# A graph network in three passes over the edges: first and second pass both with 15 sorted blocks and 44 gathered groups instead of 14 and 48

## The chip, the cores and the metric

The kernel runs on one core of a Trainium2 chip. Its five engines work side by side and wait for each other only through semaphores: TensorE (PE, matrix products into PSUM), VectorE (DVE), ScalarE (ACT), GpSimd (POOL, which here issues the gathers), and SyncE (SP, which issues all other transfers). The metric is the device time of one execution in microseconds; the kernel before has a median of 1861.92 us over three runs (1856.38 to 1866.67).

## The reference

There are 6250 nodes with 128 features and 106,250 directed edges, sorted by destination; each edge has one of 16 types. Cut to what matters:

```python
h = relu(layernorm(x))
for W, b in ((W1, b1), (W2, b2)):            # first and second pass over the edges
    s = segment_sum(h[src] @ W.T + b, dst);  h = s / max(count(dst), 1)
    h = relu(h) if W is W1 else h
x = x + h
h = relu(layernorm(x))
m = relu(concat(h[src], emb[type]) @ msg_W.T + msg_b)      # third pass
a = segment_sum(m, dst) / max(count(dst), 1)
x = x + layernorm(h + a @ upd_W.T + upd_b) * ln_g + ln_b
```

## The kernel before

**Edges, groups and blocks.** The sorted edges are padded to 104 groups of 1024. Each of the three passes has to fetch, for every edge, the row of its source node, and to sum these rows by destination. It does so in two ways at once. The first `NB[layer]` blocks of four groups (4096 edges) are sorted by the 128-node tile of their source, so that PE can pick the rows out of the node table in SBUF (`htab`) with a one-hot matrix. The remaining `NG[layer]` groups are gathered from a table in HBM by POOL. `NB = (14, 14, 13)` and so `NG = (48, 48, 52)`; `FIRST`, `OFF`, `GOFF` follow from them.

**A block.** It has `BUCKETS` = 52 buckets, one for each of 49 source tiles and 3 for what spills over, dealt out to `U` = 8 units of 7 or 6 buckets. For each bucket PE multiplies a one-hot of 128 sources (`src_hot`) with a tile of `htab` (`pick`: 384 columns, since a row is kept as three bf16 parts that add up to its fp32 value), ACT copies the result out of PSUM (L1135, tile `picked` in `region_a`), and PE sums it by destination with three products of 256 columns (`slot_sum`). DVE makes the one-hots of sources (L2038) and destinations (L1590 in the first pass, L2051 after), and at the end of a block adds its window of 256 destinations to `agg` (`last_adds`, `window_add`, L1989). There are four PSUM slots for picks.

**Sorting.** It is done once, in the first pass: while block b is summed, the tables of block b+1 and b+2 are made (`sort_*`, `digits_of`) by DVE, with small products on PE (`sort_before`, `sort_table`, `sort_turn`, `block_digits`, `block_count`) and one large copy on ACT (`tile_rows`, L1108, before the evacuations of unit 3). SP stores a block's codes (`store_codes`) to `src_tab` and `type_tab`, from which every pass loads them (L670). Edges that do not fit a block's window or buckets, or a group's window, are marked in `far` by a chain of DVE instructions after the last block of the first pass (L2138 to L2194). If any is marked, a fallback over all groups runs (the `If` branches); on these inputs none is.

**A gathered group.** POOL issues 8 indirect DMAs of 128 rows (`gather`, L829) into one of two buffers. It may start group k when the sum of group k-2 is done (`summed`). PE multiplies the rows with a one-hot of the destinations (8 x 3 products, in the first pass 8 more for the counts), DVE adds the window of 128. Group k has its place at the end of unit `place(layer, k) = (k+1) * NB * U // NG - 1` of the pass, so groups are spread evenly over the blocks. All engines' programs are written out in this order and follow it strictly.

**Early units.** The nodes are divided into 14 units of 4 or 3 tiles for the work after a pass. `early_units` lets a unit start during the second and third pass as soon as the blocks or groups that can reach it are behind: 10 of 14 in the second pass, each with products, transposes and products on PE spread over 8 units of the schedule (`early_products`), and copies on ACT (`early_sources`) and DVE (`early_rows`). The four others come after the pass. The third pass starts when the tables made there are complete: POOL needs the table in HBM, PE needs `htab`, which SP loads in part from `parts_tab` (L740).

Of the kernel before, what the change touches and what calls it, by code (L numbers as in the profile page):

```python
# [25 lines left out]
P = 128  # L26
C = 8
# [8 lines left out]
def gnn_program(nc, N, x, src, dst, first_dst, etype_cols, etype, W1T, b1, W2T, b2, embT, msgWT, msg_b,  # L36
# [16 lines left out]
    NB = (B + 1, B + 1, B)  # L53
    OFF = (0, B + 1, 2 * (B + 1))
# [4 lines left out]
    BLOCK_COLS = (B + 1) * BLOCK_C  # L59
# [17 lines left out]
    K3 = 3  # L77

    ctx = ExitStack()
    with ctx:  # L80
# [6 lines left out]
        def sems(name, n):  # L87
# [9 lines left out]
        src_tab = nc.dram_tensor("src_tab", (B + 1, BUCKETS, P), bf16, kind="Internal").ap()  # L97
        type_tab = nc.dram_tensor("type_tab", (B + 1, BUCKETS, P), bf16, kind="Internal").ap()
# [52 lines left out]
        type_f = sb("type_f", [P, 3, F])  # L151
        type_p = sb("type_p", [P, K3, F], bf16)
# [6 lines left out]
                 for h in hot]  # L159
        src_in = [sb(f"src_in{s}", [P, J * P], bf16) for s in range(2)]  # L160
# [418 lines left out]
        def _(sp):  # L579
# [96 lines left out]
            for layer in range(LAYERS):  # L676
                def step(b, first):
                    c = Count(sp, layer, b, first)
                    for u in range(U):
# [19 lines left out]
                        if layer == 0 and u == U - 1 and b < B:  # L699
                            store_codes(b + 1, b + 2)  # L700
# [76 lines left out]
            sp.wait_ge(code_T_stored, 32 * (B + 1))  # L777
# [126 lines left out]
        def _(act):  # L904
# [216 lines left out]
            for layer in range(LAYERS):  # L1121
                def step(b, first):
                    c = Count(act, layer, b, first)
                    for u in range(U):
                        if layer == 0 and u == 3 and b + 2 <= B:
# [44 lines left out]
        def _(pe):  # L1170
# [126 lines left out]
            for layer in range(LAYERS):  # L1297
# [37 lines left out]
                def step(b, first):  # L1335
# [3 lines left out]
                    for u in range(U):  # L1339
# [18 lines left out]
                        if layer == 0 and u == 5 and b < B:  # L1358
# [109 lines left out]
        def _(dve):  # L1468
# [66 lines left out]
            def split_over_partitions(value, p0, p1, p2, f0, f1, mask, to):  # L1535
# [17 lines left out]
            types_i = far[:, 0:BLOCK_COLS].bitcast(i32)  # L1553
            block_src, block_rel = src_all[:, 0:BLOCK_COLS], rel[:, 0:BLOCK_COLS]
# [14 lines left out]
                    lambda: V.tensor_tensor(float_c[:, 0:BC], dst_all[:, B * BC:(B + 1) * BC],  # L1569
                                            base_all[:, FIRST_GROUP:FIRST_GROUP + 1].broadcast_to([P, BC]), ALU.subtract),  # L1570
                    lambda: V.tensor_copy(rel_last[:, :], float_c[:, 0:BC]),
                    lambda: V.tensor_single_scalar(float_c[:, 0:BC], rel_last[:, :], 0.0, op=ALU.is_ge),
                    lambda: V.scalar_tensor_tensor(out=float_c[:, 0:BC], in0=rel_last[:, :], scalar=float(WIN_B - 1),
                                                   in1=float_c[:, 0:BC], op0=ALU.is_le, op1=ALU.mult),
                    lambda: V.scalar_tensor_tensor(out=codes[:, 1, B * BC:], in0=rel_last[:, :], scalar=1.0,
                                                   in1=float_c[:, 0:BC], op0=ALU.add, op1=ALU.mult),
# [402 lines left out]
            for layer in range(LAYERS):  # L1979
# [43 lines left out]
                def main(b, first):  # L2023
# [56 lines left out]
                    for u in range(U):  # L2080
# [10 lines left out]
                        if layer == 0:  # L2091
                            if u == 0:
                                if b < B:
                                    own = sort_codes(b + 1, 0)
                                make_digit_hot(b)
                            elif u == 1 and b < B:
                                sort_codes(b + 1, 1, own)
                                if b + 2 <= B:
                                    sort_tiles(b + 2)
                            elif u == 2 and b < B:  # L2100
# [253 lines left out]
```

## Time and profile before

| | |
|---|---|
| median of three runs | 1861.92 us |
| profiled execution | 1866.55 us |
| its span, first to last instruction | 1864.8 us |
| mean granted clock of TensorE, share of full | 0.969 |
| busy: PE | 1618.7 us (87%) |
| busy: DVE | 1365.2 us (73%) |
| busy: POOL | 1292.3 us (69%) |
| busy: ACT | 982.2 us (53%) |
| first pass, first to last matmul of a block | 93.1 to 652.6 us |
| second pass | 696.0 to 1206.4 us |
| third pass, from its first matmul | 1243.6 us on |

Matmuls are pipelined, so a busy PE need not be at its peak. Waits are named by what ended them. "issue" before a gather is the time between two instructions of POOL in which the profile shows no wait.

### The profile page before, as it was taken

What the parts mean: (1) busy time and instruction counts of PE and PEld (TensorE: products, weight loads), DVE (VectorE), ACT (ScalarE), POOL (GpSimd) and SP (SyncE); (2) the same over time, 40 slices, a digit from 0 to 9 for tenths busy, and PEclk for the clock granted to TensorE, in tenths of its full rate; (3) what the DMA queues carried; (4) which work ended last, traced back from release to release, by engine and by line L of the source; (5) the groups of instructions that cost most, each with busy time, mean ns of one, the idle gap of its engine ahead of it and who ended that gap; (6) DMA issues with size and microseconds to landing.
All of it is one profiled execution on the core that took longest, in us unless ns stands there. A gap on an engine that the chain in (4) does not pass through costs nothing.

```text
span 1864.8 us, 42446 instructions
## 1 busy us (share of the span) xinstructions
PE 1618.7 (87%) x15761; PEld 1377.4 (74%) x15761; DVE 1365.2 (73%) x3742; ACT 982.2 (53%) x1951; POOL 1292.3 (69%) x1318
## 2 busy tenths in 40 slices
PE   0189989989999967999999899849999999999996
PEld 0067777877777755777777777648998988899895
DVE  6767878878887463566666666467788888898886
ACT  3656666757766545777777777532222222222322
POOL 2087777777777617777777777657777776677772
PEclk9999999999999978999999999959999999999998
DMA  3334434344444336445555555636566666666662
GB/s 107 121 97 115 119 107 112 107 116 123 119 114 111 104 115 182 129 130 142 161 142 144 150 136 150 168 118 171 172 198 174 171 189 170 174 175 182 176 171 76
DMA packets 160332, 262.92 MB, mean 141 GB/s; under 512 B 30949, under 2 KB 126775, under 8 KB 160119
## 3 DMA queue, kind: packets, MB, share of 16 engines
q1 hardware_dynamic: 109944, 157.28, 28.6%
q0 software_dynamic: 50176, 102.84, 21.8%
q8 instruction: 130, 2.13, 0.5%
q14 instruction: 82, 0.67, 0.1%
HBM read 236.89 MB, written 23.11 MB: 139 GB/s over the span
## 4 chain that ended last, share of the span: by engine, by line
POOL 28%; PE 16%; issue 12%; DVE 4%; DMA 3%; ACT 1%; DVEq 0%; POOLq 0%
POOL rows L829 28%; PE banks L1172 16%; DMA rows<-table,src_all 3%; DVE region_a L2051 1%; DVE region_a L2257 0%; DVE htab L2262 0%; DVE agg L1989 0%; POOL region_b L842 0%; DVE rows L2077 0%; DVE x_or_cnt L1775 0%; DVE src_hot L2038 0%; DVE region_b L1976 0%; DVE stats L1800 0%; DVEq L1983 0%; DVE region_b L2036 0%
## 5 line engine op out<-in xcount | busy, mean ns | idle before, releaser
L829 POOL DMA_INDIRECT rows<-table,src_all x1184 | 1236.5, 1044 | 479.1 <-issue 440.1
L1172 PE MATMUL banks<-region_a 128*128 128x256 bf16 (+2 forms) x6168 | 1018.6, 291 | 2.3 <-DVE region_a L1590 2.3
L1135 ACT ACTIVATE region_a<-banks 128x384 bf16<-128x384 f32 x1456 | 671.7, 500 | 326.8 <-PE banks L1172 326.5
L1172 PEld LDWEIGHTS banks<-region_a 128*128 128x128 bf16 (+2 forms) x6168 | 691.8, 118 | 154.7 <-issue 4.7
L1172 PE MATMUL banks<-htab,src_hot 128*128 128x128 bf16 (+2 forms) x3484 | 631.6, 267 | 65.5 <-DVE src_hot L2038 32.9
L1172 PEld LDWEIGHTS banks<-htab,src_hot 128*128 128x128 bf16 x3484 | 288.7, 99 | 123.3 <-ACT region_a L1135 45.5
L1172 PE MATMUL banks<-hot,rows 128*128 128x128 bf16 (+1 forms) x3136 | 254.9, 239 | 63.1 <-DMA rows<-table,src_all 56.7
L1172 PEld LDWEIGHTS banks<-hot,rows 128*128 128x128 bf16 (+1 forms) x3136 | 240.8, 125 | 76.5 <-issue 54.3
L2038 DVE TENSOR_SCALAR src_hot<-src_in,part_no 128x768 bf16<-128x768 bf16 (+1 forms) x328 | 147.8, 452 | 130.6 <-PE banks L1172 115.4
L2051 DVE TENSOR_SCALAR region_a<-columns,slot_dst 128x256 f32<-128x256 f32 x676 | 210.6, 378 | 0.0
L1142 ACT ACTIVATE region_a<-banks 128x896 f32<-128x896 f32 (+1 forms) x104 | 88.9, 855 | 192.2 <-PE banks L1172 186.6
L1172 PE MATMUL banks<-type_rows,region_b 128*128 128x128 bf16 x1092 | 179.5, 221 | 0.8 <-DVE region_b L1976 0.7
L1989 DVE TENSOR_TENSOR agg<-agg,banks 128x128 f32 (+1 forms) x189 | 58.9, 312 | 159.3 <-PE banks L1172 115.9
L2051 DVE TENSOR_SCALAR region_a<-columns_b,slot_dst 128x256 bf16<-128x256 bf16 x728 | 155.4, 298 | 18.3 <-PE banks L1172 18.0
L1147 ACT ACTIVATE rows<-rows 128x1024 f32<-128x1024 f32 x52 | 55.0, 1057 | 200.8 <-DVE rows L2077 200.8
L2077 DVE TENSOR_TENSOR rows<-banks,rows 128x1024 f32<-128x1024 f32 x52 | 63.6, 1224 | 95.4 <-PE banks L1172 50.4
L1590 DVE TENSOR_TENSOR region_a<-columns_b,slot_dst 128x1792 bf16<-128x1792 bf16 (+1 forms) x112 | 113.8, 1016 | 10.5 <-PE banks L1172 10.5
L1172 PEld LDWEIGHTS banks<-type_rows,region_b 128*128 128x128 bf16 x1092 | 93.5, 99 | 7.0 <-DVE region_b L1976 1.5
L1590 DVE TENSOR_TENSOR hot<-columns_b,rel_pairs 128x1024 bf16<-128x1024 bf16 x96 | 65.5, 682 | 0.0
L1768 DVE TENSOR_TENSOR hot<-columns,rel 128x1024 f32<-128x1024 f32 x52 | 64.8, 1246 | 0.0
L1612 DVE TENSOR_TENSOR_SCAN region_b<-region_b 128x442 f16<-128x442 f16 (+1 forms) x56 | 54.0, 1007 | 2.3 <-ACT region_b L1108 2.2
L2036 DVE TENSOR_SCALAR region_b<-region_b,type_no 128x896 bf16<-128x896 bf16 (+1 forms) x104 | 53.6, 515 | 1.6 <-DMA region_b<-type_tab 1.6
(214 smaller groups left out, 1080.0 us busy)
## 6 DMA issues: line engine op xcount, KB each, us to landing
src_in<-src_tab SPq DMA_DIRECT2D x164, 224.0 KB, 3.4
src_in<-src_tab SPq DMA_DIRECT2D x164, 192.0 KB
region_b<-in_etype SPq DMA_DIRECT2D x52, 512.0 KB, 6.0
rows<-table,src_all POOLq DMA_INDIRECT x1184
region_b<-type_tab SPq DMA_DIRECT2D x52, 224.0 KB, 5.3
region_b<-type_tab SPq DMA_DIRECT2D x52, 192.0 KB
table<-htab SPq DMA_DIRECT2D x14, 384.0 KB, 3.4
table<-htab SPq DMA_DIRECT2D x14, 288.0 KB, 3.6
```

The source lines that it names most:

```text
L829: nc.gpsimd.indirect_dma_start(out=to[:, c, :], out_offset=None, in_=tab[layer], in_offset=bass.IndirectOffsetOnAxis(ap=cols[:, c:c + 1], ...
L1135: nc.scalar.activation(picked[u % 2][:, j, :], pick_ps[t % 4], ACT.Copy)\
L1142: nc.scalar.activation(messages[u % 2][:, 0:m, :], message_ps[u % 2][:, 0:m, :], ACT.Relu)\
L1147: nc.scalar.activation(rows_f[gi % 2], rows_f[gi % 2], ACT.Relu).then_inc(msgs_ready[gi], 1)
L1172: return nc.tensor.matmul(to, left, right, start=start, stop=stop)
L1590: return V.tensor_tensor(twos(to), twos(numbers), pairs.unsqueeze(2).broadcast_to([P, n, size // 2, 2]), op)
L1612: steps.done(V.tensor_tensor_scan(flat(ranks_ext[:, own, :]), flat(scan_mask[:, 0:own.stop - own.start, :]), flat(tile_ext[:, own, :]), 0. ...
L1768: return V.tensor_tensor(to, (columns if layer == 2 else columns_b)[:, :].unsqueeze(1).broadcast_to([P, C, P]), cols.unsqueeze(2).broadcas ...
L1989: V.tensor_tensor(agg[:, window], agg[:, window], ps, ALU.add).then_inc(added, 1)
L2038: V.tensor_scalar(src_hot[s][:, 0:m * P], src_in[s][:, 0:m * P], part_no[:, 0:1], None, ALU.is_equal)\
L2051: last = V.tensor_scalar(to[u % 2][:, j, :], numbers[:, :], slot_dst[:, b * BUCKETS + t:b * BUCKETS + t + 1], None, ALU.is_equal)
L2077: V.tensor_tensor(rows_f[gi % 2], type_ps, rows_f[gi % 2], ALU.add).then_inc(pre_ready[gi], 1)
```

## The change

The number of sorted blocks is 15 in the first and in the second pass (`NB = (B + 2, B + 2, B)`), so 44 groups are gathered in each, and the places of the groups follow. What was written for one block beyond the 13 common ones (`B + 1`) is written for `EXTRA` = 2 of them: the tables, the destinations relative to a block's first node (`rel_last`), and the marks of far edges. Two scratch tiles of the setup (`type_f`, `type_p`) move into halves of `hot` that the first two passes do not use, which makes room. ACT waits once, before the second table is made, for the last stored codes.

```diff
-    NB = (B + 1, B + 1, B)
-    OFF = (0, B + 1, 2 * (B + 1))
+    NB = (B + 2, B + 2, B)
+    OFF = (0, NB[0], NB[0] + NB[1])
+    SORTED = max(NB)
+    EXTRA = SORTED - B
...
-    BLOCK_COLS = (B + 1) * BLOCK_C
+    BLOCK_COLS = SORTED * BLOCK_C
...
-        slot_dst = sb("slot_dst", [P, (B + 1) * BUCKETS])
+        slot_dst = sb("slot_dst", [P, SORTED * BUCKETS])
...
-        rel_last = sb("rel_last", [P, BLOCK_C])
-        far_block = sb("far_block", [P, BLOCK_C])
-        far_group = sb("far_group", [P, BLOCK_C])
+        rel_last = sb("rel_last", [P, EXTRA * BLOCK_C])
+        far_block = sb("far_block", [P, EXTRA * BLOCK_C])
+        far_group = sb("far_group", [P, EXTRA * BLOCK_C])
...
-        type_f = sb("type_f", [P, 3, F])
-        type_p = sb("type_p", [P, K3, F], bf16)
...
+        type_f = hot[0][:, C // 2:C // 2 + 3, :]
+        type_p = hot[1][:, C // 2:C, :].rearrange("p c f -> p (c f)").bitcast(bf16)[:, 0:K3 * F].rearrange("p (k f) -> p k f", f=F)
...
+                        elif layer == 1 and b >= NB[0] and u == 0:
+                            sp.wait_ge(code_T_stored, 32 * (b + 1))
...
             def make_rows():
 
                 act.wait_ge(rinv_ready, 1)
+                act.wait_ge(code_T_stored, 32 * SORTED)
...
-                        if layer == 0 and u == 2 and b + 2 <= B:
+                        if layer == 0 and u == 2 and b + 2 < SORTED:
                             sort_before(b + 3)
-                        if layer == 0 and u == 3 and b < B:
+                        if layer == 0 and u == 3 and b + 1 < SORTED:
                             sort_table(b + 2)
...
-                here = rel_last[:, :] if b == B else rel[:, b * BC:(b + 1) * BC]
+                here = rel_last[:, (b - B) * BC:(b - B + 1) * BC] if b >= B else rel[:, b * BC:(b + 1) * BC]
...
-                    own, beyond = mask[:, 0:BC], spare[:, 0:BC]
-                    chained(lambda: V.tensor_copy(far_group[:, :], far[:, last]),
+                    own, beyond = mask[:, 0:EXTRA * BC], spare[:, 0:EXTRA * BC]
+                    now = (NB[0] - B) * BC
+                    chained(lambda: V.tensor_copy(far_group[:, :], far[:, extra]),
...
-                            lambda: V.tensor_copy(far[:, last], far_block[:, :]),
+                            lambda: V.tensor_copy(far[:, B * BC:B * BC + now], far_block[:, 0:now]),
```

The queue of POOL from the start of its first gathers to the end of the first pass; a gather is an indirect DMA of 128 rows, `x_or_cnt` holds the counts. Before, and then with the change:

```order
L829 DMA rows<-table,src_all 128x384 x16
L870 MEMSET x_or_cnt 128x6528
L829 DMA rows<-table,src_all 128x384 x368
L874 TENSOR_LOAD flag
L874 ISA x2
```

```order
L833 DMA rows<-table,src_all 128x384 x16
L874 MEMSET x_or_cnt 128x6528
L833 DMA rows<-table,src_all 128x384 x336
L878 TENSOR_LOAD flag
L878 ISA x2
```

32 gathers, four groups, are gone; the clearing of the counts still stands behind the second group.

PE in the first block of the first pass, from the sorting product of unit 3 (128x104) on. `hot,ones_b` is a group's count and `hot,rows` its sum; `htab,src_hot` is a pick and `region_a 128x256` the slot sums of a bucket; `region_a,ones` is the block's count at unit 4. Before:

```order
L1172 MATMUL banks<-region_b 128x104 x32
L1172 MATMUL banks<-hot,ones_b 128x128 x8
L1172 MATMUL banks<-hot,rows 128x128 x24
L1172 MATMUL banks<-htab,src_hot 128x384
L1172 MATMUL banks<-region_a 128x256 x3
```

With the change, the same product, and then the end of unit 4:

```order
L1177 MATMUL banks<-region_b 128x104 x32
L1177 MATMUL banks<-htab,src_hot 128x384
L1177 MATMUL banks<-region_a 128x256 x3
...
L1177 MATMUL banks<-region_a 128x256 x6
L1177 MATMUL banks<-region_a,ones 128x256
L1177 MATMUL banks<-hot,ones_b 128x128 x8
L1177 MATMUL banks<-hot,rows 128x128 x24
```

The second group has moved from the end of unit 3 to the end of unit 4; the groups of the first two blocks stood at units 1, 3, 6, 8, 10, 13, 15 and stand at 1, 4, 7, 9, 12, 15.

PE in the second pass, at the end of its fourth block. `w,agg` are the products that open an early unit; `TENSOR_LOAD first_tile` begins the next block. Before:

```order
L1172 MATMUL banks<-w,agg 128x128 x4
L1172 MATMUL banks<-hot,rows 128x128 x24
L1172 MATMUL banks<-region_a 128x256 x18
L1337 TENSOR_LOAD first_tile
L1337 ISA x2
L1172 MATMUL banks<-htab,src_hot 128x384 x7
L1172 MATMUL banks<-wm,region_b 128x128 x4
```

With the change:

```order
L1177 MATMUL banks<-hot,rows 128x128 x24
L1177 MATMUL banks<-region_a 128x256 x18
L1342 TENSOR_LOAD first_tile
L1342 ISA x2
L1177 MATMUL banks<-htab,src_hot 128x384 x7
L1177 MATMUL banks<-wm,region_b 128x128 x4
```

The early unit that opened here (number 8, four tiles) is no longer early and is done after the pass; unit 12, also of four tiles, is early instead and opens at unit 107 of 120. The numbers of early units, 10 in the second pass and 11 in the third, stay.

## Rows read from the trace of the kernel before

**Rows 1.** Windows of the two passes: stretch, length, busy us per engine, PEclk, DMA share, GB/s.

```profile
93.10:652.60 559.50, 523.53 (x5750) 422.94 (x5748) 436.92 (x939) 372.94 (x740) 433.93 (x381) 0.98 0.41 112
...
696.00:1206.40 510.40, 462.41 (x4239) 371.86 (x4239) 302.65 (x1173) 368.20 (x813) 382.35 (x384) 0.98 0.54 146
```

**Rows 2.** Waits in the first pass: who waited for what, us in total, times, longest.

```profile
POOL rows L829 <- issue: 115.7, 380, 0.3
PE banks L1172 <- DMA rows<-table,src_all: 17.4, 11, 3.2
```

**Rows 3.** Waits in the second pass.

```profile
POOL rows L829 <- issue: 125.0, 384, 8.2
PE banks L1172 <- DMA rows<-table,src_all: 39.3, 22, 7.5
```

**Rows 4.** Windows of instructions on the gathered rows, from the third group on, and second pass.

```profile
116.90:644.00 527.10, 73.43 (x1104) 66.90 (x1104) 0.00 (x0) 0.00 (x0) 413.87 (x368) 0.98 0.42 114
697.90:1197.10 499.20, 75.02 (x1128) 69.37 (x1128) 0.00 (x0) 0.00 (x0) 382.35 (x384) 0.98 0.54 146
```

**Rows 5.** Timeline of PE, first pass: start, us, engine, line, operation.

```profile
308.88 0.62 PE L1172 MATMUL banks<-hot,ones_b 128*128 128x128 bf16 x8
...
310.68 0.33 PE L1172 MATMUL banks<-htab,src_hot 128*128 128x384 bf16 x1
...
311.17 0.33 PE L1172 MATMUL banks<-htab,src_hot 128*128 128x384 bf16 x1
```

**Rows 6.** Timeline of DVE: adds of finished blocks in the first pass.

```profile
183.50 0.42 DVE L1989 TENSOR_TENSOR agg<-agg,banks 128x256 f32 x1 [1.48 <-PE banks L1172]
...
221.42 0.42 DVE L1989 TENSOR_TENSOR agg<-agg,banks 128x256 f32 x1 [1.45 <-PE banks L1172]
...
265.62 0.42 DVE L1989 TENSOR_TENSOR agg<-agg,banks 128x256 f32 x1 [1.51 <-PE banks L1172]
...
302.82 0.42 DVE L1989 TENSOR_TENSOR agg<-agg,banks 128x256 f32 x1 [1.42 <-PE banks L1172]
...
574.80 0.42 DVE L1989 TENSOR_TENSOR agg<-agg,banks 128x256 f32 x1 [0.56 <-issue]
...
611.38 0.42 DVE L1989 TENSOR_TENSOR agg<-agg,banks 128x256 f32 x1 [1.47 <-PE banks L1172]
```

**Rows 7.** Windows at low clock, end of first and start of second pass (PEclk 0.50).

```profile
634.80:641.60 6.80, 5.95 (x39) 4.66 (x40) 0.49 (x2) 1.47 (x3) 5.08 (x6) 0.50 0.30 80
...
733.80:740.50 6.70, 5.34 (x36) 4.31 (x37) 0.29 (x1) 1.32 (x3) 4.87 (x7) 0.50 0.95 289
```

**Rows 8.** Timeline of DVE: adds of finished blocks in the second pass.

```profile
745.02 0.42 DVE L1989 TENSOR_TENSOR agg<-agg,banks 128x256 f32 x1 [1.10 <-PE banks L1172]
...
776.91 0.42 DVE L1989 TENSOR_TENSOR agg<-agg,banks 128x256 f32 x1 [2.04 <-issue]
...
847.64 0.42 DVE L1989 TENSOR_TENSOR agg<-agg,banks 128x256 f32 x1 [1.69 <-PE banks L1172]
...
883.31 0.42 DVE L1989 TENSOR_TENSOR agg<-agg,banks 128x256 f32 x1 [1.21 <-PE banks L1172]
...
917.16 0.42 DVE L1989 TENSOR_TENSOR agg<-agg,banks 128x256 f32 x1 [1.87 <-PE banks L1172]
```

**Rows 9.** Groups by line and shape, PE, second pass.

```profile
L1172 PE MATMUL banks<-wm,region_b 128*128 128x128 f32 x70 | 9.4, 275 | 0.0
```

**Rows 10.** Timeline of DVE after the last block of the first pass.

```profile
654.84 0.18 DVE L2165 COPY far_group<-far 128x32 f32<-128x32 f32 x1
...
658.16 0.27 DVE L2188 TENSOR_TENSOR region_b<-region_b,limits 128x104 f32<-128x104 f32 x1
```

**Rows 11.** Timeline of SP and PE, end of second pass and start of third.

```profile
1203.56 4.86 SPq L740 DMA_DIRECT2D htab<-parts_tab  x10
...
1243.63 0.50 PE L1172 MATMUL banks<-htab,src_hot 128*128 128x128 bf16 x3 [3.73 <-DVE src_hot L2038]
```

**Rows 12.** The page, costliest groups: evacuations on ACT.

```profile
L1135 ACT ACTIVATE region_a<-banks 128x384 bf16<-128x384 f32 x1456 | 671.7, 500 | 326.8 <-PE banks L1172 326.5
```

More of the change, by code:

```diff
@@ L698, in step @@
                             sp.dma_start(xres, x_v).then_inc(x_in, 16)
-                        if layer == 0 and u == U - 1 and b < B:
+                        if layer == 0 and u == U - 1 and b + 1 < SORTED:
                             store_codes(b + 1, b + 2)
@@ L776, in _ @@
                 sp.wait_ge(out_stored[k], 16 * len(range(k, NV, 3)))
[L777 removed]
+            sp.wait_ge(code_T_stored, 32 * SORTED)
         @block.gpsimd
@@ L1124, in step @@
                     for u in range(U):
-                        if layer == 0 and u == 3 and b + 2 <= B:
+                        if layer == 0 and u == 3 and b + 2 < SORTED:
                             tile_rows(b + 3)
@@ L1357, in step @@
                             block_count(b)
-                        if layer == 0 and u == 5 and b < B:
+                        if layer == 0 and u == 5 and b + 1 < SORTED:
                             sort_turn(b + 2)
@@ L1568, in _ @@
                                                    op0=ALU.add, op1=ALU.mult),
[L1569 to L1576, printed above, removed]
+                    lambda: V.tensor_tensor(by_block(float_c[:, 0:EXTRA * BC]), by_block(dst_all[:, extra]),
+                                            first_of_block(base_all), ALU.subtract),
+                    lambda: V.tensor_copy(rel_last[:, :], float_c[:, 0:EXTRA * BC]),
+                    lambda: V.tensor_single_scalar(float_c[:, 0:EXTRA * BC], rel_last[:, :], 0.0, op=ALU.is_ge),
+                    lambda: V.scalar_tensor_tensor(out=float_c[:, 0:EXTRA * BC], in0=rel_last[:, :], scalar=float(WIN_B - 1),
+                                                   in1=float_c[:, 0:EXTRA * BC], op0=ALU.is_le, op1=ALU.mult),
+                    lambda: V.scalar_tensor_tensor(out=codes[:, 1, extra], in0=rel_last[:, :], scalar=1.0,
+                                                   in1=float_c[:, 0:EXTRA * BC], op0=ALU.add, op1=ALU.mult),
                     lambda: V.memset(scan_mask, 1.0),
@@ L2168, in _ @@
                                                            op0=ALU.is_gt, op1=ALU.max),
-                            lambda: V.scalar_tensor_tensor(out=far_block[:, :], in0=rank1[:, last], scalar=float(2 * P),
+                            lambda: V.scalar_tensor_tensor(out=far_block[:, :], in0=rank1[:, extra], scalar=float(2 * P),
                                                            in1=far_block[:, :], op0=ALU.is_gt, op1=ALU.max),
-                            lambda: V.tensor_tensor(own, tile_no[:, last, 0], first_tile[:, FIRST_GROUP:FIRST_GROUP + 1]
-                                                    .broadcast_to([P, BC]), ALU.subtract),
+                            lambda: V.tensor_tensor(by_block(own), by_block(tile_no[:, extra, 0]), first_of_block(first_tile), ALU.subtract),
                             lambda: V.tensor_single_scalar(beyond, own, 0.0, op=ALU.is_lt),
@@ L2175, in _ @@
                                                            op0=ALU.is_gt, op1=ALU.max),
-                            lambda: V.scalar_tensor_tensor(out=beyond, in0=rank1[:, last], scalar=float(P), in1=beyond,
+                            lambda: V.scalar_tensor_tensor(out=beyond, in0=rank1[:, extra], scalar=float(P), in1=beyond,
                                                            op0=ALU.is_gt, op1=ALU.mult),
                             lambda: V.tensor_tensor(far_block[:, :], far_block[:, :], beyond, ALU.max),
-                            lambda: V.scalar_tensor_tensor(out=own, in0=dst_all[:, last], scalar=1.0, in1=far_block[:, :],
+                            lambda: V.scalar_tensor_tensor(out=own, in0=dst_all[:, extra], scalar=1.0, in1=far_block[:, :],
                                                            op0=ALU.add, op1=ALU.mult),
                             lambda: V.tensor_single_scalar(far_block[:, :], own, -1.0, op=ALU.add),
-                            lambda: V.tensor_copy(far[:, last], far_block[:, :]),
+                            lambda: V.tensor_copy(far[:, B * BC:B * BC + now], far_block[:, 0:now]),
                             lambda: V.reduce_max(far_max[:, 1:2], far_block[:, :], axis=AX.X),
@@ L2206, in _ @@
                     if layer == 2:
-                        V.tensor_copy(far[:, B * BC:(B + 1) * BC], far_group[:, :]).then_inc(far_swapped, 1)
+                        V.tensor_copy(far[:, extra], far_group[:, :]).then_inc(far_swapped, 1)
                         dve.wait_ge(far_swapped, 1)
```

33 lines of the change are left out of this document (18 added, 15 removed).

## The prediction

> **What bounds the kernel now.** I read the busy times of the two stretches that the change touches, then who waits for whom in each, and last the timelines of TensorE (PE) and of VectorE (DVE). The matmuls of the first pass fill 559.5 us of the profile and those of the second 510.4 us, with PE, the busiest engine, at work for 94% and 91% of it [rows 1]. The reader is to see a second engine without slack beside PE: in both passes GpSimd (POOL) waits for nothing between its gathers but 0.3 us of its own issue, 380 and 384 times (the one of 8.2 us stands before the first gather of the second pass) [rows 2, 3]. A group of 8 gathers takes 527.1/46 = 11.5 us in the first pass and 499.2/48 = 10.4 us in the second [rows 4]. So POOL sets the pace of the passes as a whole: the 48 groups need 48 times that, and PE, which is nearly as slow, catches up with them and waits, 17.4 us in the first pass [rows 2] and 39.3 us in the second [rows 3]. Some of these waits cost twice: behind the longest the granted clock stands at 0.50 (1.2 GHz) for 3 to 7 us while PE works, and half of that time is lost [rows 7]. A block gives POOL nothing to do; a gathered group costs PE little. The change trades one for the other in both passes, so the question is whether PE has room for what POOL gives up.
>
> **What PE pays for each.** In a dense stretch of the first pass the count and the sum of one group take 310.68 - 308.88 = 1.80 us, and one bucket (its pick and three slot sums) 311.17 - 310.68 = 0.49 us [rows 5]. A block has 52 buckets, 25.5 us, and in the first pass also its sorting. The change adds a block (25.5 us at the least) and takes away four groups (7.2 us in the first pass, 8 counts each less in the second, about 5.4 us). PE's own work thus grows by about 20 us in each pass, and POOL's shrinks by 4 x 11.5 = 46 us and 4 x 10.4 = 42 us [rows 4]. POOL then stops being the bound, and what is saved is only what PE waits for gathers today.
>
> **First pass, block by block.** The add of a finished block's 256 columns comes once a block, so the distance of two such adds is a block's time. With three groups and no wait for a gather it is 221.42 - 183.50 = 37.9 and 302.82 - 265.62 = 37.2 us; four more such blocks gave 37.2 to 37.9, mean of the six 37.7 [rows 6]. Their groups did not wait, so this is PE's own pace, with its small waits for ScalarE (ACT) and DVE in it. The new plan has 44 groups on 15 blocks: three in each, but two in the sixth. Sum: the first block 45.6 as now (its stall is for the clearing of the counts behind the second group, which stays); twelve blocks of 37.7 less one group, 450.6; the last block but one 611.38 - 574.80 = 36.6 as its counterpart now [rows 6]; the last, which has nothing to sort, from its counterpart: 652.6 - 611.4 + 1.0 (the add follows the last slot sum by that much) = 42.2, less one group 1.8, less its two gather waits 3.8 (a part of the 17.4) and less half of 6.8 us at the low clock [rows 7] = 33.2. Together 566 us, against 559.5: **+6 us**. The gathers need 44 x 11.5 = 506 us of it and are no longer late. Bounds: if the twelve blocks all take the 36.6 of the quickest with three groups [rows 6], the pass comes to 566 - 12 x 1.1 = 553, -7; if every block takes the 37.9 of the slower ones and a gather wait of 2 us stays in three of them, +14. I take the blocks as measured.
>
> **Second pass.** Without a wait for a gather and without work of an early unit (the last stage of a finished range of nodes, done between the blocks) a block with four groups takes 776.91 - 745.02 = 31.9 us, so 30.5 with three. With such work in it and almost no gather wait: 883.31 - 847.64 = 35.7 and 917.16 - 883.31 = 33.9 [rows 8], and two more of 34.9 and 33.5, mean 34.5. These four hold somewhat more than their share of the early units' matmuls, which come to about 24 us in the pass (three kinds, one of the two larger 9.4 us [rows 9]) and stay the same in number: 35 tiles of nodes, one unit of four dropped and another of four added at the end. Spread over the twelve blocks from the fourth to the fifteenth they give 33.9. Sum: first block 48.0 now, less its second and third gather wait 4.6 and half of the 6.7 us at the low clock behind the third [rows 7], 40.0 (the wait for the very first gather, 7.5 us, stays); two of 30.5; twelve of 33.9; less one group 1.3. Together 506 us against 510.4: **-4 us**. Gathers: 44 x 10.4 = 458 us, no bound. Bounds: if the waits for gathers go and nothing takes their place, 510.4 + 25.5 - 5.4 - 31.8 (39.3 less the first 7.5) - 6.6 (half of 6.7 [rows 7] and of two stretches of 3.3 us at the low clock behind them) = 492, -18; if the twelve blocks all take the 35.7 of the slowest, +18. I choose near the middle because the blocks without gather waits are the longer ones for their content: there PE meets ACT, whose waits are hidden behind a late gather today.
>
> **The small terms.** After the first pass the marking of far edges runs on DVE while PE waits for it. Fourteen of its instructions go from 32 to 64 columns: 0.18 us at 32 and 0.27 us at 104 [rows 10], so 0.04 us each, +0.5 us. The same at the start, and 480 instead of 448 columns in ten instructions: +0.3 us, on the path, since the first pick waits for DVE. The scratch of the type rows moves to another buffer: same instructions, nothing. The added wait of ACT for the stored codes stands behind the last of 15 stores, issued a block earlier, with the whole making of the second table behind it: nothing; were the store late, its landing would be added. At the end of the second pass the last early unit now ends in the last block, so its parts are stored after it and the ten loads of the third table, issued at 1203.56 now, start some 4 us later; the third pass begins at 1243.63 [rows 11], which covers that. The third pass is the same program.
>
> **Sum.** +6 + 0.5 + 0.3 - 4 = +3 us. The profiled execution took 1866.6 us with a span of 1864.8; it is 4.6 us over the median of the runs, so I add the difference to the median: 1861.9 + 3 = 1865, rounded towards the lower bounds, which reach further, to **1864 us**.
>
> **Rivals.**
> Faster, because nothing takes the place of the gather waits: PE closes up, the ACT waits do not come back. For it: PE's matmuls stand back to back in the row of buckets [rows 5]. Against: the blocks of the first pass above had no gather wait and still took 37.7 [rows 6]. With -18 in the second pass and -2 in the first (blocks of 37.0), 1862 - 20 = 1842 us.
> Slower: ACT's waits decide the second pass. Its evacuation of a bucket takes 0.50 us [rows 12], level with PE's 0.49, and each early unit puts other work in its queue. A late gather lets ACT catch up today; without one every such block may cost 35.7 us [rows 8]. Point of turning: 510.4 = 40.0 + 61.0 + 12x - 1.3 gives x = 34.2 us; above it the pass is longer than before. At 35.7 it is +18, with the first pass +6: 1887 us.
> Gathers still the bound of the first pass: three of them are longer than a block of 37.7 from 12.6 us a group on. The step from the second pass to the first, where DVE is busier (437 of 559.5 us against 303 of 510.4 [rows 1]), is 1.1 us a group [rows 4]; one and a half such steps more make 13.2 us a group and 39.6 a block, 1.9 us more in each of twelve: +23, 1887 us. Against it: a block of the new plan has no more DVE work than one with three groups has now. The Trainium skill (SBUF — State Buffer, Who interferes with whom) says that DVE in some of its modes locks GpSimd out of a port that it needs to write a gather's descriptors. The trace agrees in that a gather instruction takes 413.87/368 = 1.12 us in the first pass and 1.00 in the second [rows 4].
> Not what it says: should one of the two sorted blocks 13 and 14 hold an edge out of its window, a fallback over all groups runs and the time is several times as long. From the inputs, these blocks span 241 and 238 nodes of the 256 and their fullest bucket beside their own holds 99 of 128, so this is excluded.
>
> **How the numbers follow.** Forecast case 0.54 (own range 1852 to 1876), faster rival 0.22, ACT rival 0.17, gathers still the bound 0.07. The range that leaves out 2 in 10 is 1846 to 1882. A measurement of this kernel can tell about 0.5%, 9 us, from no change. Faster by more: the faster rival and a little of the forecast case, 0.27; slower by more: the two slow ones and a little of the forecast case, 0.27; within: 0.46.
>
> **What would show it.** POOL waits for PE between groups in both passes, several us a group; PE's waits for gathers fall to a few us in the first pass and below 15 in the second; block adds 37 to 38 us apart in the first pass; around 34 in the second. Wrong if the block distances of the first pass fall to 36 or less, if the second pass is under 495 or over 520 us, or if gather waits stay as they are.

## The result and the profile after

The changed kernel takes 1848.38 us (median of 9 runs, 1845.76 to 1852.65), the kernel before on the same chip 1858.21 us (9 runs, 1854.97 to 1866.67): a ratio of 0.9942 with the interval 0.9923 to 0.9960. The forecast was 1864 us. The time lies in the range, but the change is a gain of 10 us where the sum said a loss of 3, and the case "faster by over 0.5%" had only 0.27. Run again on another chip the ratio was 0.9942 (0.9928 to 0.9956).

The windows of the two passes in the changed kernel; the columns are those of [rows 1].

```profile
92.90:658.20 565.30, 538.10 (x5930) 433.79 (x5930) 459.21 (x987) 399.67 (x793) 396.28 (x350) 0.99 0.40 108
701.60:1194.40 492.80, 475.40 (x4351) 384.15 (x4351) 311.59 (x1226) 391.09 (x865) 350.12 (x352) 0.98 0.55 148
```

The first pass went from 559.5 to 565.3 us, +5.8, and the forecast was +6. The second went from 510.4 to 492.8 us, -17.6, and the forecast was -4: the miss is all in it. The prediction named a second pass under 495 us as a sign that it is wrong. PE is now at work for 96% of the second pass, where it was for 91%.

Who waits for what, first pass and then second; they answer to [rows 2] and [rows 3].

```profile
POOL rows L833 <- issue: 99.8, 327, 0.5
POOL rows L833 <- PE banks L1177: 56.3, 22, 6.1
PE banks L1177 <- DMA rows<-table,src_all: 1.2, 1, 1.2
```

```profile
POOL rows L833 <- issue: 110.5, 335, 8.2
POOL rows L833 <- PE banks L1177: 25.1, 17, 4.1
PE banks L1177 <- DMA rows<-table,src_all: 9.0, 2, 7.4
PE banks L1177 <- ACT region_a L1140: 2.8, 4, 1.4
```

In both passes POOL now waits for PE, which it did not before, and PE's waits for gathers fell from 17.4 to 1.2 us and from 39.3 to 9.0 us, 7.4 of it at the start of the second pass. A gather costs what it did: the windows that answer to [rows 4] give 376.70/336 = 1.12 and 350.12/352 = 0.99 us, as 1.12 and 1.00 before; in the first pass that is so although DVE is busier than it was (459 of 565.3 us against 437 of 559.5).

```profile
116.30:645.00 528.70, 62.47 (x999) 57.55 (x1000) 0.00 (x0) 0.00 (x0) 376.70 (x336) 0.99 0.41 111
703.70:1181.20 477.50, 64.82 (x1017) 61.37 (x1018) 0.00 (x0) 0.00 (x0) 350.12 (x352) 0.98 0.55 148
```

The block adds on DVE, first pass, as in [rows 6]: three blocks with three groups, one with two, and the last but one.

```profile
181.18 0.42 DVE L1998 TENSOR_TENSOR agg<-agg,banks 128x256 f32 x1
...
218.54 0.42 DVE L1998 TENSOR_TENSOR agg<-agg,banks 128x256 f32 x1
...
255.73 0.42 DVE L1998 TENSOR_TENSOR agg<-agg,banks 128x256 f32 x1 [1.09 <-PE banks L1177]
...
292.93 0.42 DVE L1998 TENSOR_TENSOR agg<-agg,banks 128x256 f32 x1 [1.24 <-PE banks L1177]
...
328.35 0.42 DVE L1998 TENSOR_TENSOR agg<-agg,banks 128x256 f32 x1 [1.11 <-PE banks L1177]
...
589.65 0.42 DVE L1998 TENSOR_TENSOR agg<-agg,banks 128x256 f32 x1 [0.54 <-issue]
...
625.52 0.42 DVE L1998 TENSOR_TENSOR agg<-agg,banks 128x256 f32 x1 [1.58 <-PE banks L1177]
```

They stand 37.4, 37.2 and 37.2 us apart, then 35.4, and 35.9 for the last but one. The adds of the second pass, as in [rows 8]:

```profile
810.99 0.42 DVE L1998 TENSOR_TENSOR agg<-agg,banks 128x256 f32 x1 [2.03 <-issue]
...
842.48 0.42 DVE L1998 TENSOR_TENSOR agg<-agg,banks 128x256 f32 x1 [1.67 <-PE banks L1177]
...
874.75 0.42 DVE L1998 TENSOR_TENSOR agg<-agg,banks 128x256 f32 x1 [1.68 <-PE banks L1177]
...
904.95 0.42 DVE L1998 TENSOR_TENSOR agg<-agg,banks 128x256 f32 x1 [1.17 <-PE banks L1177]
...
936.16 0.42 DVE L1998 TENSOR_TENSOR agg<-agg,banks 128x256 f32 x1 [1.20 <-PE banks L1177]
...
1163.66 0.42 DVE L1998 TENSOR_TENSOR agg<-agg,banks 128x256 f32 x1 [1.17 <-PE banks L1177]
```

31.5, 32.3, 30.2, 31.2 us, and from the first shown to the last 352.7/11 = 32.1 us a block. The forecast had 33.9 less a tenth.

**How steady a pass is.** Each kernel's stretches, read as the distance from the first pick of a pass to its last (so some 4 us less than the windows above), from all profiles taken on chips where the kernel before takes about 1860 us; "way" is the stretch between passes, "tail" what is behind the last pick; all in us, to about 0.1. The kernels of the lower rows are those of the next section.

| kernel | pass 1 | way | pass 2 | way | pass 3 | tail |
|---|---|---|---|---|---|---|
| before | 555.5 | 47.5 | 506.8 | 40.8 | 592.2 | 29.0 |
| before, again | 557.4 | 46.8 | 501.5 | 43.8 | 590.3 | 29.0 |
| changed | 561.2 | 47.4 | 489.1 | 42.3 | 589.3 | 28.7 |
| changed, again | 558.6 | 47.6 | 489.0 | 41.8 | 587.4 | 28.6 |
| second half alone | 550.0 | 48.2 | 489.8 | 43.2 | 589.1 | 31.3 |
| first half alone | 558.2 | 47.9 | 501.5 | 46.4 | 588.4 | 34.6 |
| first half, again | 561.3 | 47.9 | 498.2 | 46.1 | 585.9 | 34.3 |
| seven gathers | 556.9 | 47.0 | 469.7 | 41.5 | 590.1 | 33.0 |
| slowed GpSimd | 557.3 | 47.8 | 518.2 | 48.7 | 588.1 | 28.6 |
| 16 blocks | 563.6 | 47.3 | 507.6 | 42.9 | 589.8 | 28.9 |
| half, units 8 apart | 552.0 | 47.9 | 489.4 | 42.4 | 588.2 | 31.3 |

The second pass of the kernel before, which waits for gathers, took 506.8 us in one execution and 501.5 in the other; that of the changed kernel, which doesn't, 489.1 and 489.0. So the gain there is 12 to 18 us, and the profile on which the forecast rests was at the long end. The two profiles of the first half alone, whose second pass has the old plan too, had 501.5 and 498.2: against the mean of all four, 502, the gain is 13 us.

### The profile page after: what moved, and what is told of

It reads as the page before. It is cut to its first block, busy times and chain, and to the rows that moved or that the text cites. A ratio compares the mean times of both kernels' runs of the same rounds, so it can differ in the third digit from the quotient of the medians.

```text
span 1850.9 us, 43216 instructions
## 1 busy us (share of the span) xinstructions
PE 1644.3 (89%) x16053; PEld 1399.4 (76%) x16053; DVE 1397.6 (76%) x3843; ACT 1032.0 (56%) x2056; POOL 1227.5 (66%) x1258
## 4 chain that ended last, share of the span: by engine, by line
PE 42%; POOL 7%; issue 5%; DVE 4%; DMA 2%; ACT 2%; DVEq 0%; POOLq 0%; ACTq 0%
PE banks L1177 42%; POOL rows L833 7%; ACT region_a L1140 1%; DMA rows<-table,src_all 1%; DMA src_in<-src_tab 1%; DVE region_a L2060 1%; DVE region_a L2265 0%; DVE htab L2270 0%; PE banks L1269 0%; DVE x_or_cnt L1784 0%; DVE stats L1809 0%; DVE agg L1998 0%; POOL region_b L846 0%; DVEq L1992 0%; DVE src_hot L2047 0%
## 5 line engine op out<-in xcount | busy, mean ns | idle before, releaser
L833 POOL DMA_INDIRECT rows<-table,src_all x1120 | 1171.6, 1046 | 521.0 <-issue 412.0
L1177 PE MATMUL banks<-region_a 128*128 128x256 bf16 (+2 forms) x6512 | 1064.5, 289 | 2.7 <-DVE region_a L1599 2.7
L1140 ACT ACTIVATE region_a<-banks 128x384 bf16<-128x384 f32 x1560 | 718.1, 500 | 267.7 <-PE banks L1177 266.0
L1177 PEld LDWEIGHTS banks<-region_a 128*128 128x128 bf16 (+2 forms) x6512 | 721.1, 117 | 161.9 <-DVE region_a L1599 4.8
L1177 PE MATMUL banks<-htab,src_hot 128*128 128x128 bf16 (+2 forms) x3588 | 663.9, 269 | 75.4 <-DVE src_hot L2047 36.2
L2047 DVE TENSOR_SCALAR src_hot<-src_in,part_no 128x896 bf16<-128x896 bf16 (+1 forms) x344 | 155.0, 452 | 143.9 <-PE banks L1177 116.0
L1177 PE MATMUL banks<-hot,rows 128*128 128x128 bf16 (+1 forms) x2944 | 235.3, 236 | 13.3 <-DMA rows<-table,src_all 10.2
L1177 PEld LDWEIGHTS banks<-hot,rows 128*128 128x128 bf16 (+1 forms) x2944 | 224.9, 125 | 19.5 <-issue 14.9
L2060 DVE TENSOR_SCALAR region_a<-columns_b,slot_dst 128x256 bf16<-128x256 bf16 x780 | 165.3, 296 | 19.0 <-PE banks L1177 18.8
L820 POOL MEMSET agg<- 128x512 f32 (+1 forms) x28 | 12.4, 472 | 62.2 <-PE banks L1177 43.4
```

Of the source, the lines that this page charges most:

```text
L833: nc.gpsimd.indirect_dma_start(out=to[:, c, :], out_offset=None, in_=tab[layer], in_offset=bass.IndirectOffsetOnAxis(ap=cols[:, c:c + 1], ...
L1140: nc.scalar.activation(picked[u % 2][:, j, :], pick_ps[t % 4], ACT.Copy)\
L1177: return nc.tensor.matmul(to, left, right, start=start, stop=stop)
L2047: V.tensor_scalar(src_hot[s][:, 0:m * P], src_in[s][:, 0:m * P], part_no[:, 0:1], None, ALU.is_equal)\
L2060: last = V.tensor_scalar(to[u % 2][:, j, :], numbers[:, :], slot_dst[:, b * BUCKETS + t:b * BUCKETS + t + 1], None, ALU.is_equal)
```

## The experiments

**Two theories.** The forecast took two things from [rows 8]: four blocks with early units and almost no gather wait had a mean of 34.5 us, and in them PE waited for ACT; it held that a late gather covers such waits elsewhere and that they come up when it is gone. Call this *cover*. The rival is *cause*: in the trace of before a late gather makes PE's group sum late, DVE's add of it late, the moments behind that late, and so ACT's std, behind which the evacuations stand in ACT's queue; then ACT's waits should go with the gather waits.

**The halves apart, on two other chips.** The first edit leaves the first pass at 14 blocks, the second the second pass. Sorting is all done in the first pass, so that of the second half alone still sorts the fifteenth block.

```diff
-    NB = (B + 2, B + 2, B)
+    NB = (B + 1, B + 2, B)
```

```diff
-    NB = (B + 2, B + 2, B)
+    NB = (B + 2, B + 1, B)
```

> NB = (14, 15, 13): only the second pass has the fifteenth block, the first keeps 14 blocks and 48 groups. Theory A (my reading of the profile after): the two passes are independent, the first one lost 5.8 us and the second one won 17.6. Then this kernel is 17 us faster than before, ratio about 0.991, first pass 559 to 560 us, second pass 493 us. Theory B (the passes are coupled, or the gain is partly the drift of the third pass from one execution to the next, 3.3 us in the two profiles): the second pass alone does not come under 500 us, or the time stays within 8 us of before.

> NB = (15, 14, 13): only the first pass has the fifteenth block. Theory A: 6 us slower than before, ratio about 1.003, first pass 565 us without waits for gathers, second pass as before, 510 us. Theory B (coupled): the second pass moves too, or the first gains what the other experiment does not show.

Measured: 1.0126 (1.0083 to 1.0170) and 0.9998 (0.9961 to 1.0036). Neither can be used for the question, for the kernel before took 2510 us on that chip instead of 1860. On a second such chip (2506 us) the same kernels gave 1.0084 (1.0044 to 1.0124) and 1.0001 (0.9973 to 1.0030).

> Second pass 15 blocks and 44 gathered groups, first pass 14 and 48, third 13 and 52: the second half of the change alone, again, on another chip than e1_second_only, whose chip ran every kernel a third slower with TensorE busy 75% of the span. If the gathers bound the second pass in the kernel before, as in its trace (gather waits 39.3 us), it takes about 493 us instead of 510.4 and the time falls by 15 to 18 us, to a ratio of 0.991. By the forecast on record it would fall by 4 us (0.998). On a chip where GpSimd waits for TensorE and not the reverse (796 us in e1_second_only) the block more can only cost: ratio 1.01 again.

Waits of the second half alone on the first of these chips, whole kernel:

```profile
POOL rows L833 <- PE banks L1177: 796.2, 125, 13.4
...
PE banks L1177 <- issue: 321.0, 410, 4.4
```

POOL waits 796 us for PE, so the gathers do not bind there and a block more has nothing to win back; that it costs was measured twice. What is seen of PE there stands at the end.

**The whole, again.** Both kernels as they are, beside each other.

> The changed kernel once more, beside the kernel before on the same chip. On a chip where the kernel before takes about 1858 us: ratio 0.994, second pass 493 us, first 565. On one of the chips on which it takes about 2506 us (the last eight runs), where GpSimd waits some 750 us for TensorE: if the two halves add up there, 1.008 times 1.000, ratio 1.008; the slowed changed kernel had 0.997 there, so if the halves don't add, 0.995.

Measured: 0.9942 (0.9928 to 0.9956), 1850.39 us, and for the kernel before against itself 0.9990 (0.9973 to 1.0007). This chip was one of 1860 us, and so were those of all runs below.

**The halves apart, where gathers bind.**

> The second half of the change alone (first pass 14 blocks and 48 groups, second 15 and 44). If the two halves are independent, the second pass takes 493 us as in the changed kernel and the first stays at 559.5: 17 us less, ratio 0.991, and this kernel beats both others. By the forecast on record 4 us less, 0.998. If the chip is one on which the kernel before takes 2506 us, ratio 1.01 as twice before, and nothing is told.

> The first half alone (15 and 44, then 14 and 48). Halves independent: first pass 565 us, second 510, 6 us more, ratio 1.003. Rival: the second pass gains from the first pass's other end, then ratio 1.000 or less.

Measured: the second half alone 1847.08 us, ratio 0.9932 (0.9917 to 0.9947); the first half alone 1872.08 us, ratio 1.0064 (1.0046 to 1.0082), and once more:

> The first half alone once more. If the 8 us between it and the sum of the parts belong to this kernel, ratio 1.006 again and the profile again long in the way to the third pass (over 45 us) and in the tail (over 33). If they belonged to the executions of that chip, ratio 1.001 to 1.003 (its first pass is 1 to 2 us longer than the two of the kernel before, its second 2 us shorter than their mean).

Measured: 1869.33 us, 1.0055 (1.0034 to 1.0075). The gain comes with the second half; the first half costs. The second pass of the first half alone still waits for gathers as before (waits of PE in it, first run):

```profile
PE banks L1177 <- DMA rows<-table,src_all: 38.0, 22, 7.5
...
PE banks L1177 <- ACT region_a L1140: 5.4, 7, 1.8
```

The halves give -13.5 and +11.5 or +8.5 us, together -2 to -5, and the whole -10 to -11.5. Most of the rest is a wait at the very end of the program, behind GpSimd's last copy, in code that no edit touches. The closing DRAIN of POOL in the kernel before, in the changed one and in the first half alone (count, then shortest, median and longest in ns):

```profile
L80 POOLq DRAIN  x1: 3731/3731/3731, 1860.9 to 1860.9; - x1
...
L82 POOLq DRAIN  x1: 6347/6347/6347, 1844.3 to 1844.3; - x1
...
L82 POOLq DRAIN  x1: 8960/8960/8960, 1861.0 to 1861.0; - x1
```

It belongs to a kernel and not to a run: 3.73 us in both profiles of the kernel before, 6.35 and 6.35 in the changed kernel, 8.96 in both of the first half alone and 8.96 in the second half alone. Without it the halves give -18.7 and +6.3 or +3.3 us, together -12.5 to -15.5, and the whole -12.5 and -14.1: they add up. Why it differs, no run here tells, nor why the way to the third pass is 4 us longer in the first half alone. The first pass of the first half alone is 3.3 us longer (means of two), less than the +6. And not all of the second half's gain is in the second pass: its first pass took 550.0 us (552.0 in the kernel with units 8 apart) against 555.5 and 557.4, though it too has 14 blocks there; 4 to 5 us of it are in the last block (37.1 us instead of 42.2 and 41.1), where it waited 1.3 us for gathers instead of 3.8 and 3.9.

**Gather waits away, blocks as before.** Seven gathers instead of eight for each group of the second pass, an eighth of its gathered rows left out, so the result is not the reference's.

```diff
+        chunks = lambda layer: 7 if layer == 1 else C
...
-                for c in range(C):
+                for c in range(chunks(layer)):
```

PE and DVE wait for as many gathers as are issued (cut here); their products stay.

> The kernel before with seven gathers of eight in each group of the second pass (an eighth of the gathered rows there is left out; products and blocks stay). Theory A (a late gather makes VectorE's group sum, then ScalarE's std, then the evacuations late, so ScalarE's waits go with the gather waits): second pass 470 us or less, ratio 0.978, waits for ScalarE under 4 us in the pass. Theory B, the forecast's (a late gather covers waits for ScalarE that come up once it is gone, 1.8 us a block): pass above 483 us, ratio over 0.985.

Measured: 1831.98 us, 0.9844 (0.9827 to 0.9862); the second pass 469.7 us. (On the two slow chips 0.9885 and 0.9848.) The pass is as short as *cause* said (470 us or less), but not the ratio (0.978), and the mechanism is neither's. Part of the ratio is a longer tail, 33.0 us for 29.0; the closing wait of POOL is 7.65 us here instead of 3.73. PE's waits in its second pass:

```profile
PE banks L1179 <- DVE src_hot L2045: 9.9, 2, 7.2
PE banks L1179 <- DMA rows<-table,src_all: 6.9, 2, 6.1
PE banks L1179 <- ACT region_a L1142: 5.3, 7, 1.8
```

and the same view of the kernel before, second pass:

```profile
PE banks L1172 <- DMA rows<-table,src_all: 39.3, 22, 7.5
PE banks L1172 <- DVE src_hot L2038: 7.2, 1, 7.2
PE banks L1172 <- ACT region_a L1135: 5.3, 7, 1.8
```

32 us of gather waits went, and with them the two stretches of 3.4 us at the low clock behind the late gathers at 1095 and 1191 us of the kernel before. The waits for ACT are 5.3 us in 7 times both with and without them. They are even the same ones. The picks that waited most for ACT, before and then with seven gathers (start, us, and in brackets the wait):

```profile
856.12 0.34 PE L1172 MATMUL banks<-htab,src_hot 128*128 128x384 bf16 x1 [1.20 <-ACT region_a L1135]
...
865.21 0.34 PE L1172 MATMUL banks<-htab,src_hot 128*128 128x384 bf16 x1 [0.72 <-ACT region_a L1135]
...
1030.56 0.34 PE L1172 MATMUL banks<-htab,src_hot 128*128 128x384 bf16 x1 [1.79 <-ACT region_a L1135]
```

```profile
846.25 0.34 PE L1179 MATMUL banks<-htab,src_hot 128*128 128x384 bf16 x1 [1.21 <-ACT region_a L1142]
...
855.34 0.34 PE L1179 MATMUL banks<-htab,src_hot 128*128 128x384 bf16 x1 [0.72 <-ACT region_a L1142]
...
1010.65 0.34 PE L1179 MATMUL banks<-htab,src_hot 128*128 128x384 bf16 x1 [1.79 <-ACT region_a L1142]
```

1.20, 0.72, 1.79 against 1.21, 0.72, 1.79 us, in the fifth, the fifth and the tenth block of both. The waits belong to those places in the order of the work; here a late gather neither covers nor causes them. The block that began with the add at 847.64 in [rows 8] took 35.7 us; here, with no gather wait anywhere near, the same block took 873.13 - 837.76 = 35.4, and the other blocks from the fourth on, by their first picks, 31.5 to 34.6.

```profile
837.76 0.42 DVE L1996 TENSOR_TENSOR agg<-agg,banks 128x256 f32 x1 [1.69 <-PE banks L1179]
...
873.13 0.42 DVE L1996 TENSOR_TENSOR agg<-agg,banks 128x256 f32 x1 [1.12 <-PE banks L1179]
```

**Gather waits back, all else as after.** Behind each group's gathers in the second pass GpSimd clears a small tile three times, and waits for it each time (cut to the lines that matter):

```diff
+                    if layer == 1:
+                        for i in range(3):
+                            nc.gpsimd.memset(idle_room[:, :], 0.0).then_inc(idle, 1)
+                            pool.wait_ge(idle, 3 * k + i + 1)
```

> The changed kernel with three small memsets on GpSimd after each group's gathers in the second pass, some 1.4 us a group more. Both theories: the gathers bind again, gather waits over 25 us in the pass (9.0 in the changed kernel). Theory A: waits for ScalarE rise from 4.6 us to 7 or more, and the pass gets longer by more than the gather waits grow. Theory B: they stay at 4.6 or fall, and the pass gets longer by the gather waits or less.

Measured: 1881.86 us, 1.0110 (1.0091 to 1.0128); the second pass 518.2 us instead of 489.1. (On a slow chip the same kernel had 0.9970, 0.9937 to 1.0004.)

```profile
PE banks L1183 <- DMA rows<-table,src_all: 33.5, 16, 7.3
PE banks L1183 <- DVE src_hot L2053: 7.2, 1, 7.2
PE banks L1183 <- ACT region_a L1146: 2.1, 3, 1.4
```

Gather waits rose by 24.5 us and those for ACT did not (2.8 before it by the same view; the 4.6 of the expectation is another count). *Cause* falls. That the pass would grow by no more than the gather waits was wrong too: it grew by 29 us, 4.6 more. Three of its stretches at the low clock, like this one, are not in the changed kernel, and at half speed they cost 1.7 us each; one of the changed kernel at the start is half as long here, which leaves about 3.4 us for the low clock:

```profile
875.80:879.20 3.40, 3.40 (x26) 2.78 (x23) 0.29 (x1) 0.00 (x0) 2.58 (x3) 0.50 0.35 92
```

**One block more still.** 16 blocks and 40 groups in the second pass, 15 and 44 in the first.

```diff
-    NB = (B + 2, B + 2, B)
+    NB = (B + 2, B + 3, B)
```

> NB = (15, 16, 13): against the changed kernel one more block and four groups fewer in the second pass. Theory A (TensorE is the bound there with 15 blocks, with hardly any wait left): the second pass grows by 25.5 + 0.5 - 5.4 = about 20 us to 513, about 10 us slower than before. Theory B (GpSimd still sets part of the pace at 15): it grows by less than 12 us.

> Second pass with 16 blocks and 40 groups, first 15 and 44, third 13 and 52. If a block for four groups costs TensorE's own time once the gathers do not bind (its busy time rose by 13.0 us from 14 to 15 blocks), the second pass takes 489 + 13 = 502 us from its first pick to its last and the ratio is 1.001. By the forecast's block price (33.9 us a block, less 5.4 for four groups' products) 489 + 28, ratio 1.009. If gathers still bind the changed kernel's pass anywhere but at its start, less than 502.

Measured: 1876.67 us, 1.0094 (1.0064 to 1.0124), the second pass 507.6 us (on a slow chip 1.0069, 1.0030 to 1.0107). Both lengths of the second expectation missed: +18.6 us for the block, neither 13 nor 28. That the ratio is near the 1.009 that went with 28 is luck, for the kernel is 26 to 28 us slower than the changed one, and 8 to 10 of these lie outside the second pass. The first expectation had +20 us and 513 us for the window, PE's own price for a block less four groups (25.5 - 5.4); the window took 511.3 against 492.8. In it PE's busy time rose by 21.5 us (475.4 to 496.95), waits for gathers fell by 4.6 and for ACT by 1.8, and those for DVE rose by 3.0.

```profile
POOL rows L833 <- PE banks L1177: 88.9, 36, 5.6
...
PE banks L1177 <- DVE src_hot L2047: 12.7, 2, 7.1
PE banks L1177 <- DMA rows<-table,src_all: 4.4, 1, 4.4
PE banks L1177 <- ACT region_a L1140: 1.0, 3, 0.6
```

POOL waits 88.9 us there. Of 14, 15 and 16 blocks, the second pass is shortest with 15.

**What makes the waits for ACT.** Early units at least 8 units apart, on the second half alone.

```diff
-        APART = 5
+        APART = 8
```

> The second half alone (14, 15, 13 blocks), with the early units of the second pass at least 8 units apart instead of 5. If ScalarE's waits come from units whose early work crowds, they fall from 6.0 us to under 4 and the kernel gains 2 us on s1_second_only (ratio 0.992); if they come from something else, 5.5 to 6.5 us stay and the ratio is 0.993 or more, as wider spacing pushes the last early unit towards the pass's end.

Measured: 1842.81 us, 0.9909 (0.9886 to 0.9932), the fastest kernel here. PE's waits in its second pass:

```profile
PE banks L1177 <- DVE src_hot L2047: 11.0, 2, 7.2
PE banks L1177 <- DMA rows<-table,src_all: 8.4, 2, 7.3
PE banks L1177 <- DVE agg L1998: 0.8, 1, 0.8
PE banks L1177 <- ACT region_a L1140: 0.4, 2, 0.2
```

The waits for ACT fall from 3.1 us to 0.4 in this view (the 6.0 of the expectation is another count), with the same number of early products: most of them come from early units that crowd. The five blocks from the ninth to the thirteenth take 161.5 us against 163.9. But the first two take 2.0 us more, with 3.4 us more at the low clock and longer waits for DVE, so the second pass takes 489.4 us against 489.8: the profile shows 0.4 us of gain and not 2, and the intervals of the two kernels overlap (0.9886 to 0.9932, 0.9917 to 0.9947). That 8 is better than 5 isn't shown. That 14, 15 and 13 blocks beat the kernel before is.

## Why the prediction was wrong

**What bounds (right).** POOL was without slack, and giving it less let PE run on: POOL waits for PE now, 56.3 and 25.1 us. With GpSimd slowed the gather waits and the time came back.

**First pass (right).** 565.3 us against 566: first block 47.5 (45.6 forecast), twelve 448.3 (450.6), the last but one 35.9 (36.6), the last 33.7 (33.2), by the first picks of the blocks. Its terms miss by +1.9 and -2.3 us, which cancel, and the second profile of each kernel makes the step +1 instead of +6, the mean +3.4: the direction is right, the exact hit is luck.

**Second pass (wrong, and this is the step that failed).** The sum had 40.0 + 61.0 + 405.5; measured 44.5 + 63.5 + 384.8. The first three blocks came out 7 us longer, because the waits and the low clock at the start stayed. The twelve others came out 20.7 us shorter: the term "twelve of 33.9" was too large. It rests on four sampled blocks of mean 34.5, and in these PE waited 1.9, 1.3, 2.2 and 1.0 us, mean 1.6, of which 1.3 for ACT: they held nearly all of the pass's waits for ACT (5.1 of the 5.3 us, in the view of the kernel before that stands with the seven gathers). The sum gave such waits to all twelve, 19.3 us; the twelve blocks of the changed kernel wait 2.2 us in all. That is 17 of the 20.7 us. The other 4 are the blocks' work: beyond the 30.5 us of a block without early work the sum had 1.8 us of it a block, and 1.5 was measured. The seven-gather kernel shows the same waits for ACT in the same four blocks and 0.2 us in all its others from the fourth on together.

The sample was chosen for having no gather wait. All four blocks have three groups. The two other blocks with three groups behind the third block have waits for ACT of 0.2 and 0.0 us, and gather waits of 2.1 and 1.7 us. This fits a simple reading: where PE loses 2 us to ACT, the gathers gain 2 us on it, so a block without a gather wait is likelier to be one with a wait for ACT. I took what the selection brought in for the pace of all blocks. The reading rests on six blocks; the sizes do not depend on it.

**The reason given (wrong).** "ACT's waits are hidden behind a late gather today": the same waits stand in the trace with 39.3 us of gather waits and with 6.9.

**Bounds and rivals.** The lower bound of the second pass, 492, was the nearest number to the 492.8 measured; in its terms the gather waits went by 30.3 us where it had 31.8, but the low clock's cost by 3.6 where it had 6.6, and other profiles put the gain at 9 to 18 us, so the nearness is partly luck. The first rival had this right and the first pass wrong (-2 for +5.8), which makes 1842 where 1848 was measured. The ACT rival needed 34.2 us a block and is out by 2 us. Gathers as a bound of the first pass: 1.2 us of waits, out.

**Small terms.** The way to the second pass took 43.4 us before and after, where +0.5 was forecast. The third pass began 1.3 us later after the second than before (38.55 for 37.2 us), where 0 was forecast. Its own 3 us less (592.2 to 589.3) are little more than the 1.9 to 2.5 us by which two executions of one kernel differ in it; what is left is not explained. The closing wait of POOL, not in the sum, costs the changed kernel 2.6 us.

## What to carry to other kernels

When two engines pace a stretch and work is moved off one, price the stretch afterwards by the other engine's own work plus the waits that you can place, one by one, and not by the mean of the blocks that happen not to wait today: these are few, and they are quick or slow for a reason. Before giving a wait to all blocks, divide its total over the pass by the number of blocks (here 5.3/14 = 0.4 us for ACT, where the sample had 1.3). And try the two halves of a change apart: here one half carried the gain and the other cost some of it. Compare stretches before totals: a closing wait that no edit touched shifted these by up to 5 us.

## What the runs showed of the hardware

- On two chips every kernel that ran there took a third longer (before: 2510 and 2506 us, against 1858 to 1862 on the others), with instructions as long as elsewhere: a gather 1012 ns in the second half alone against 1046 in the changed kernel, an evacuation on ACT 497 against 500. What grew was idle time: ACT's before its evacuations is 792 us in the second half alone there, and 268 us in the changed kernel elsewhere. In the slowed kernel on such a chip PE's pick at 1308.24 is followed by ACT's copy only at 1310.56 and by the next pick at 1311.10:

```profile
1308.24 0.34 PE L1183 MATMUL banks<-htab,src_hot 128*128 128x384 bf16 x1 [0.30 <-issue]
...
1310.56 0.49 ACT L1146 ACTIVATE region_a<-banks 128x384 bf16<-128x384 f32 x1 [2.38 <-remote]
...
1311.10 0.50 PE L1183 MATMUL banks<-htab,src_hot 128*128 128x384 bf16 x1 [2.20 <-issue]
```

  "remote" is a releaser that the profile does not name, so what delays it stays open. The sign of a change can turn with the chip: the second half alone was 0.9932 on one kind and 1.0084 and 1.0126 on the other.
- Waits that belong to the order of the work repeat to 0.01 us between two kernels whose profiled times differ by 34 us (1.20, 0.72, 1.79 against 1.21, 0.72, 1.79).
- Stretches that no edit touches differed between kernels and repeated within one: tails of 28.7 and 28.6 us (changed), 29.0 and 29.0 (before), 34.6 and 34.3 (first half alone). The closing DRAIN on GpSimd is a part of them: 3.73 us in three profiles (before, before again, 16 blocks), 6.34 to 6.35 in three (changed, changed again, slowed GpSimd), 7.65 in one (seven gathers), 8.96 in four (both halves, first half again, units 8 apart).
